# A recurrence and a routed expert layer on one core: the second state part made directly, tanh in two halves, x products, weight pieces and low parts moved

## The reference

```python
def step(h, xt):
    m = jnp.concatenate([xt, h], axis=-1) @ weight + bias     # (64, 512) @ (512, 512)
    c = jnp.tanh(m[:, 256:])
    g = jax.nn.sigmoid(m[:, :256] + 1.0)
    h_new = g * h + (1.0 - g) * c
    return (h_new, h_new)
...
gate_logits = gate_in @ gate_w + gate_b      # from means over steps of x
# two experts of four for each batch; a mask by step for experts 1 and 2
h = gelu(context_c @ ew1[e] + eb1[e]); y = h @ ew2[e] + eb2[e]
out = out + w_be[:, e][:, None, None] * mask[e][None, :, None] * y
shared = gelu(context_c @ sw1 + sb1) @ sw2 + sb2
return x + out + shared
```

## Time and profile before

| | us |
|---|---|
| median of 3 runs | 661.3 |
| the profiled execution | 663.13 |
| its span in the trace | 661.4 |
| TensorE busy | 642.6 (97%) |
| VectorE busy | 415.1 (63%) |
| ScalarE busy | 314.5 (48%) |
| GpSimd busy | 259.9 (39%) |

### The profile page before, as it was taken

How to read it: one execution, slowest core, us unless ns; L and a number is a source line. 1 busy time by engine, 2 the same in 40 slices (tenths; PEclk the granted TensorE clock), 3 DMA queues, 4 the chain that set the end, 5 groups by cost and what they waited for, 6 DMA issues and landing times.

```text
span 661.4 us, 16521 instructions
## 1 busy us (share of the span) xinstructions
PE 642.6 (97%) x5828; PEld 557.7 (84%) x5828; DVE 415.1 (63%) x947; ACT 314.5 (48%) x537; POOL 259.9 (39%) x514
## 2 busy tenths in 40 slices
PE   7799999999999999999999999999999999999995
PEld 4699888888888888888878888888888899999995
DVE  5788987556566655668747644554456785555554
ACT  5454454343443343444647544444446664554460
POOL 1467775544554454433345333123311443311300
PEclk9999999999999999999999999999999999999998
DMA  7510210000000000000002100000001310000006
GB/s 258 205 53 10 58 49 18 0 1 0 0 0 0 0 0 0 1 1 2 1 2 81 48 0 0 0 0 0 0 0 58 94 58 0 0 0 0 0 1 255
DMA packets 7751, 20.74 MB, mean 31 GB/s; under 512 B 800, under 2 KB 1056, under 8 KB 7200
## 3 DMA queue, kind: packets, MB, share of 16 engines
q1 hardware_dynamic: 7424, 19.59, 8.6%
q10 hardware_dynamic: 288, 0.64, 0.3%
HBM read 16.03 MB, written 4.19 MB: 31 GB/s over the span
## 4 chain that ended last, share of the span: by engine, by line
PE 92%; DVE 3%; DMA 1%; issue 1%; ACT 1%; POOL 1%; DVEq 0%; SPq 0%; ACTq 0%; POOLq 0%
PE zy L882 56%; PE hp L882 37%; DMA acc<-in_x 1%; DVE d_t L552 0%; DVE d_t L550 0%; POOL g_lo L370 0%; ACT uc L407 0%; DVE acc L827 0%; DVE h_b L555 0%; DVE h_r L540 0%; DVE y_all L755 0%; DVE h_b L542 0%; ACT g_hi L426 0%; DVE first L559 0%; DVE w_buf L533 0%
## 5 line engine op out<-in xcount | busy, mean ns | idle before, releaser
L527 DVE TENSOR_TENSOR g_lo<-g_f,g_hi 128x512 fp32r<-128x512 f32 (+2 forms) x172 | 127.7, 743 | 156.1 <-ACT g_hi L426 153.8
L882 PE MATMUL zy<-g_hi,w_buf 128*128 128x512 f32 (+2 forms) x736 | 186.6, 375 | 0.5 <-issue 0.5
L426 ACT ACTIVATE g_hi<-g_f 128x512 fp32r<-128x512 f32 (+2 forms) x184 | 109.9, 597 | 152.2 <-PE zy L882 151.8
L419 ACT ACTIVATE g_f<-hp,first 128x512 f32<-128x512 f32 (+3 forms) x188 | 122.9, 654 | 117.8 <-PE hp L882 113.2
L882 PE MATMUL hp<-shared_buf,w_buf 128*128 (+1 forms) x720 | 173.6, 376 | 0.0
L882 PEld LDWEIGHTS hp<-shared_buf,w_buf 128*128 128x128 f32 x720 | 135.0, 188 | 19.0 <-issue 0.3
L882 PEld LDWEIGHTS zy<-g_hi,w_buf 128*128 128x128 f32 x736 | 132.1, 188 | 19.7 <-ACT g_hi L426 0.7
L882 PEld LDWEIGHTS zy<-h_b,y_all 128*128 128x128 bf16 x3072 | 93.9, 98 | 21.5 <-issue 13.1
L882 PE MATMUL zy<-g_lo,w_buf 128*128 128x512 f32 (+2 forms) x368 | 107.6, 373 | 0.9 <-POOL g_lo L370 0.9
L882 PE MATMUL zy<-h_b,y_all 128*128 128x64 bf16 x3072 | 102.7, 193 | 5.8 <-DVE h_b L555 5.3
L882 PE MATMUL hp<-x_hl,w_buf 128*128 (+2 forms) x432 | 104.9, 378 | 0.7 <-POOL x_hl L312 0.7
(11 more groups left out here) (126 smaller groups left out, 455.2 us busy)
## 6 DMA issues: line engine op xcount, KB each, us to landing
stage<-in_w_exp SPq DMA_DIRECT2D x40, 256.0 KB, 2.9
out_y<-acc SPq DMA_DIRECT2D x2, 1376.0 KB, 4.7
acc<-in_x SPq DMA_DIRECT2D x1, 2048.0 KB, 7.7
acc<-in_x SPq DMA_DIRECT2D x1, 1536.0 KB, 10.0
out_y<-acc SPq DMA_DIRECT2D x1, 1344.0 KB, 5.5
acc<-in_w SPq DMA_DIRECT2D x1, 512.0 KB, 4.7
acc<-in_x SPq DMA_DIRECT2D x1, 512.0 KB, 6.9
acc<-in_w ACTq DMA_DIRECT2D x1, 512.0 KB, 5.6
```

What stands on the lines that cost most here:

```text
L419: act.activation(raw_of(j, n, keep), hp[j % 2][:, 0:n], ACT.Gelu_apprx_tanh, bias=par[:, S_B1 + e * NCH + j:S_B1 + e * NCH + j + 1]).then_ ...
L426: act.activation(chunk_of(j, n, keep)[0], raw_of(j, n, keep), ACT.Copy).then_inc(ghi_done, 1)
L527: dve.tensor_tensor(lo, raw_of(j, n, keep), hi.bitcast(F32), ALU.subtract).then_inc(glo_done, 1)
L882: return pe.matmul(out_, lhsT=lhsT, rhs=rhs, start=start, stop=stop, skip_group_check=True)
```

## The change

- The second part is subtracted directly, h - h_b[:, 0] into bfloat16, ahead of h_r, in all steps. It no longer waits for h_r.
- The state products go through m in the order 2, 3, 0, 1 (`C_FIRST`), so the columns of c are complete first; in steps 0 to 11 (`APART`) that raises `c_done`, ScalarE makes the tanh of c and of g as two instructions, and the cell's first instruction waits for c's alone.
- In group 0 the x products stand in steps 0, 1, 2, 3 (one each) and 4 (two), 5, 6 (one each), directly behind the state products; in group 1 one in every step. At step 0 the high parts of x are used first and the low ones behind a wait for POOL. POOL makes the low part of x of step 15 before its last sum of group 0.
- Weight pieces 5, 6, 7 move from steps 5, 6, 7 to 6, 8, 9.
- VectorE makes the low parts of chunks 66, 67, 68 (`DVE_LOW`) after 2, 5 and 8 of the gather copies; POOL leaves them out.

```diff
+APART = GT + QT
+C_FIRST = [2, 3, 0, 1]
+PIECE_AT = {0: 0, 1: 1, 2: 2, 3: 3, 4: 4, GT - 2: 5, GT: 6, GT + 1: 7}
+X_PARTS = [[[0], [1], [2], [3]], [[0, 1], [2], [3], []]]
+DVE_LOW = {6: 2, 7: 5, 8: SLOTS}
...
+            pool.wait_ge(xa_hi, GT)
+            x_low(2 * GT - 1)
             head_low(GT - 2)
             add_h(GT - 1, GT - 1)
-            pool.wait_ge(xa_hi, GT)
-            x_low(2 * GT - 1)
...
             for c in range(T - QT, NS * NCH):
+                if c - T + QT in DVE_LOW:
+                    continue
                 n = width(c // NCH)
-                if c == T - QT:
+                if c == T - QT or c - 1 - T + QT in DVE_LOW:
                     pool.wait_ge(glo_done, c)
...
+            def tanh(s, i, buf, apart=False):
+                if apart:
+                    act.wait_ge(c_done, s + 1)
+                    act.activation(uc[:, 1], zb[:, buf, 1, :, i % QT, :], ACT.Tanh).then_inc(tanh_c, 1)
+                    act.wait_ge(z_done, s + 1)
+                    act.activation(uc[:, 0], zb[:, buf, 0, :, i % QT, :], ACT.Tanh).then_inc(tanh_done, 1)
...
-                piece_high(i)
+                if i in PIECE_AT:
+                    piece_high(PIECE_AT[i])
...
                 gelu_chunk(q, j, E, width(q))
+                if s in PIECE_AT:
+                    piece_high(PIECE_AT[s])
...
                 dve.wait_ge(h_done, s + 2)
+                dve.tensor_tensor(h_b[:, 1], h, h_b[:, 0], ALU.subtract).then_inc(h2_done, 1)
                 dve.tensor_tensor(h_r[:], h, h_b[:, 0], ALU.subtract).then_inc(hr_done, 1)
                 dve.wait_ge(hr_done, s + 2)
-                dve.tensor_copy(h_b[:, 1], h_r[:]).then_inc(h2_done, 1)
                 dve.wait_ge(h2_done, s + 2)
...
+                if apart:
+                    dve.wait_ge(tanh_c, s + 1)
+                else:
+                    dve.wait_ge(tanh_done, s + 1)
                 dve.wait_ge(h_done, s + 1)
                 dve.tensor_tensor(d_t[:], h_f[:, i % 2], uc[:, 1], ALU.subtract).then_inc(d_done, 1)
                 dve.wait_ge(d_done, s + 1)
+                if apart:
+                    dve.wait_ge(tanh_done, s + 1)
...
+                for j, upto in DVE_LOW.items():
+                    for s in range(at, upto):
...
+                        last = dve.tensor_copy(dst, tokens_of(x_hl, ORDER[1], bs[s]))
...
+                    at, c = upto, T - QT + j
+                    dve.wait_ge(glo_done, c)
+                    split_lo(c // NCH, c % NCH, width(c // NCH))
...
+                if low:
+                    for k in range(K):
+                        for w in range(2):
+                            mm(o, wx[:, w, k, c], x_hl[:, 0, k, bass.ds(s, QT), :], False)
+                    pe.wait_ge(xs_done, low)
+                    for k in range(K):
+                        mm(o, wx[:, 0, k, c], x_hl[:, 1, k, bass.ds(s, QT), :], False)
+                    return
...
-                    for m in range(2 * K):
+                    for m in C_FIRST:
...
+                        if apart and a == 2 and m == 2 * K - 1:
+                            last.then_inc(c_done, 1)
                 last.then_inc(z_done, 1)
...
+                    if head != 0 and j:
+                        if head == 1 and i == 0:
+                            pe.wait_ge(piece_done, 6)
+                        layer1(q, j, w_of(0), group_src(q), width(q))
+                    if not (last_group and i >= QT):
+                        if i % QT == 0:
+                            pe.wait_ge(seeded, 2 * g + 1 + i // QT)
+                            if head == 0 and i == 0:
+                                pe.wait_ge(x4_hi, 1)
+                            else:
+                                pe.wait_ge(xs_done, s + QT)
+                        for m in X_PARTS[i // QT][i % QT] if head == 0 else [i % QT]:
+                            x_part(s - i % QT + QT, (i // QT + 1) % 2, m, QT if head == 0 and i == 0 else None)
```

More of the change, by code:

```diff
@@ L403, in seed @@
                                bias_z.unsqueeze(2).to_broadcast([P, 2 * K, QT * B]), ACT.Copy).then_inc(seeded, 1)
[L405 to L408, removed]
+            def tanh(s, i, buf, apart=False):
[5 more added lines that the diff above has]
+                else:
+                    act.wait_ge(z_done, s + 1)
+                    act.activation(uc[:],
+                                   zb[:, buf, :, :, i % QT, :], ACT.Tanh).then_inc(tanh_done, 1)
                 if i % QT == QT - 1:
+                    if apart:
+                        act.wait_ge(tanh_c, s + 1)
                     act.wait_ge(tanh_done, s + 1)
@@ L459, in _ @@
             for i in range(GT):
[L460 removed]
+                tanh(i, i, i // QT, True)
                 act.activation(x_hl[:, 0, :, GT + i, :], acc[:, :, GT + i, :], ACT.Copy).then_inc(xa_hi, 1)
@@ L613, in _ @@
             for i in range(GT):
-                cell(i, i, i < 2)
-                piece_low(i)
+                cell(i, i, i < 2, True)
+                if i in PIECE_AT:
+                    piece_low(PIECE_AT[i])
                 for j in first_chunks(i):
@@ L623, in _ @@
                     shared_out(0, yp)
-                cell(s, i)
+                cell(s, i, apart=s < APART)
                 split_lo(q, j, width(q))
+                if s in PIECE_AT:
+                    piece_low(PIECE_AT[s])
                 if s >= GT + QT:
@@ L911, in h_first, with h_part @@
                     for a in range(3 - b):
-                        for m in range(2 * K):
+                        for m in C_FIRST:
                             for k in range(K):
                                 last = mm(zb[:, 0, m // 2, m % 2, 0, :], wh[:, b, k, m * P:(m + 1) * P], h_b[:, a, k], False, b == 2)
+                            if b == 2 and m == 2 * K - 1:
+                                last.then_inc(c_done, 1)
                 last.then_inc(z_done, 1)
-            def h_part(s, i, buf):
+            def h_part(s, i, buf, apart=False):
                 for a, ready in enumerate((h1_done, h2_done, h3_done)):
                     pe.wait_ge(ready, s + 1)
-                    for m in range(2 * K):
+                    for m in C_FIRST:
                         o = zb[:, buf, m // 2, m % 2, i % QT, :]
@@ L998, in steps @@
                     else:
-                        h_part(s, i, i // QT)
+                        h_part(s, i, i // QT, head is not None and s < APART)
                     q, j = chunk_at(g, i)
+                    if head != 0 and j:
[7 more added lines that the diff above has]
+                                pe.wait_ge(x4_hi, 1)
+                            else:
+                                pe.wait_ge(xs_done, s + QT)
+                        for m in X_PARTS[i // QT][i % QT] if head == 0 else [i % QT]:
+                            x_part(s - i % QT + QT, (i // QT + 1) % 2, m, QT if head == 0 and i == 0 else None)
                     if head == 0:
@@ L1007, in steps @@
                             layer1(0, j, w_of(0), group_src(0), width(0), j < 2)
-                    elif j:
-                        if head == 1 and i == 0:
-                            pe.wait_ge(piece_done, 6)
-                        layer1(q, j, w_of(0), group_src(q), width(q))
-                    if not (last_group and i >= QT):
-                        if i % QT == (0 if head is None else 1):
-                            pe.wait_ge(seeded, 2 * g + 1 + i // QT)
-                            pe.wait_ge(xs_done, s - i % QT + QT)
-                        for m in [i % QT] if head is None else ([], [0], [1], [2, 3])[i % QT]:
-                            x_part(s - i % QT + QT, (i // QT + 1) % 2, m)
                     if head != 0 and j == 0:
```

17 lines of the change are left out of this document (9 added, 8 removed).

## The result

| | before | after |
|---|---|---|
| median, runs on the same chip | 661.5 (6 runs, 661.02 to 663.5) | 659.0 (6 runs, 658.96 to 659.06) |
| the profiled execution | 663.13 | 659.06 |
| its span | 661.4 | 657.3 |
| TensorE busy | 642.6 (97%) | 641.0 (98%) |
| VectorE busy | 415.1 (63%) | 420.5 (64%) |

The ratio is 0.995, interval 0.9937 to 0.9962: faster by 0.5%, more than the 0.2% that a measurement of this kernel can tell. The forecast was 656.7 us, with a range of 654.8 to 659.3 that holds the 659.0. The runs of the kernel before lie on two levels, near 661.3 and near 663.0, and its profiled execution is from the upper one; the kernel after has one level.

What follows compares the result with a forecast made beforehand. TensorE was taken to bound the kernel, its long middle full, so only stalls around it could be won. Head 3.0 plus gather 1.6 made 4.6 us, off the median of 661.3: 656.7 us, range 654.8 to 659.3.

Steps and rivals of the forecast that it cites:

- C: Between recurrence and experts: the gather stall stays, its cause not the port or VectorE's low parts late; 658.3 us, chance 0.07.
- F: Steps 0 to 3 and 7: c_done comes late, keeping 0.3 us a step, 1.5 in all; 658.2 us, chance 0.06.
- Gather, 1.6: Between recurrence and experts: VectorE making low parts of chunks 66 to 68 saves 1.6 us, bounds 0.9 to 1.8.
- Head, 3.0: From the start: 2.65 us saved by step 12, about 0.35 more around step 14; bounds 1.2 and 4.2.
- Tanh: Early recurrence steps: halves of 0.30 us, the second 0.2 to 0.28 behind, make step 2's q 0.3 us sooner.
- Rival B: Steps 0 to 3 and 7: tanh halves do not overlap, 0.78 us a pair, 1.0 us less gain; 657.7 us, chance 0.08.
- Step 3's pin: Step 3: weight piece 2, landing at 22.27, holds cell 3 until 23.64, 0.5 us late; step 4's products start at 24.8.
- The wait for x's low part: Step 4: two x products wait for POOL's low part, 2.85 us after the step's start; step 5 starts at 29.1.
- Steps 8 to 11: VectorE takes over as the bound: 4.4 us in steps 8 and 9, 3.67 in 10 and 11; step 12 at 55.5.
- rival D: Steps 5 to 14: VectorE's subtractions and POOL hold each other off, cells 0.3 us longer; about 659.7 us, chance 0.09.
- A: Steps 8 to 11: VectorE does not bind, its instructions beside POOL shrink; head 4.2 us, total 655.5 us, chance 0.16.
- E: Steps 5 to 14: VectorE steps grow, deciding from 0.46 us each; at 0.65 us slower, 663.2 us, chance 0.04.

Runs made afterwards that it cites:

- experiments 2: The kernel before with only the low parts of chunks 66 to 68 moved to VectorE among the gather copies: 661.13 us, ratio 0.9969.
- experiment 4: The kernel before with VectorE waiting for POOL's low parts after the second and fifth gather copy, POOL keeping all low parts: 661.17 us, ratio 0.9995.
- head alone: The changed kernel without the gather part, so POOL makes the low parts of chunks 66 to 68 again: 661.33 us, ratio 0.9965.
- experiment 6: The changed kernel with one piece undone each time: whole tanh 660.0 us, second part copied from h_r 659.07, weight pieces back 658.84, x products back 660.76.

## Why the prediction was right, and where it was not

**The bound** was read rightly: the middle stays full, and a microsecond saved in the head or the gather reaches the last products whole (2.54 and 1.84 make 4.37).

**The last step of the sum failed.** I took 4.6 us, worked out on an execution of 663.13, from a median of 661.3. The miss of 2.3 us is 1.8 of this and 0.5 of the terms: for the profiled execution the forecast was 658.5, and it took 659.06. The stall of the earlier trace rows was priced rightly, but as if each run had it, though the table of the front showed a profiled execution 1.5 us above the highest run of the median. If the lower level is without the stall (experiments 2 and 4), only the head is left there: 661.3 less 2.54, of which the tail hands 0.36 back, is 659.1. Where before lies at 663.0, after's 659.0 is 4.0 us less.

**That 659.0 lies in the range is luck in part.** It is 0.3 us inside the upper end, 659.3, and the gain is 2.3 to 2.5 us where 4.6 was forecast. The upper end was set for costs such as longer VectorE steps beside POOL (head 1.2), a gather stall that stays (C, 658.3) or a late c_done (F, 658.2), and none of these came at that size. A stall that is missing from the runs of the median was on no list.

**Gather, 1.6:** 1.85. I held back the 0.47 "issue" of the earlier trace rows; it went as well. Rival C is out. POOL's 2.83 us outlasted the rest of the train, more than five copies of 0.39 us, and with the train broken it took 0.74. The Trainium skill, "SBUF — State Buffer", SBUF: two separate sides, says that the loser of the shared port waits for the winner's whole instruction. A wait of one copy does not give this row; that one side waits for a whole instruction of the other does agree with the copies of 0.96 and 0.94 us in experiment 4.

**Head, 3.0:** 2.54 (head alone), 2.56 by step 16 counted from step 0. By its steps:
- Tanh: 0.28 us for a half and 0.17 between starts, close to the 0.30 and 0.2 taken. Rival B is out: the pair takes 0.44 us. The Trainium skill's budget ("ScalarE: Activation LUTs", Rules for kernel authors), from which the prediction estimated 0.82 us for the pair, is stated for an activation whose bias is a pointer operand. The tanh here has none and takes 0.28 and 0.39 us; the gelu, which has one, takes 0.48 for 256 columns, near the 0.51 of that budget. But I put the gain in steps 0 to 3 and 7. By step 8 only 0.45 had come, as the pin of step 3 took 0.28 back, and 0.79 more came behind it, where I had VectorE bound by its own work and the tanh of no account.
- The loop: 3.28 to 3.41 less 0.46 is 2.8 to 2.95, not the 2.9 to 3.0 written. Steps 1 and 2 took 2.95 and 3.08.
- Direct part: 0.16 a step in steps 1 to 3, as taken. What I had not looked at is the end of the program, where a gap of 0.36 us appeared; it is not this part's doing alone (experiment 6).
- Step 3's pin: right in kind, mis-sized. Piece 2 came at 22.50 for 22.27, VectorE's low part took 0.90 and d 0.54 us, so step 4 began at 25.24 for 24.8.
- The wait for x's low part: at 28.26 for 27.65, and step 5 at 29.76 for 29.1. Of these 0.61 us, 0.44 come from step 4, which starts later. The other 0.17 is that TensorE starts 3.02 us behind step 4's products and not 2.85: POOL's low part ends 2.88 behind them (28.12), and TensorE starts 0.14 later. POOL's addition ahead of it (L313, at 26.39) takes 0.79 us, no more than before:

```profile
27.13 0.79 POOL L307 TENSOR_TENSOR acc<-acc,first 128x128 f32<-128x128 f32 x1 [1.89 <-DVE h_b L544]
```

- The pin and this wait make the 0.5 us missing at step 12 (2.18 for 2.65), and 0.44 more by step 16 was near the 0.35 taken.
- Steps 8 to 11: cells at 38.85, 42.27, 46.06, 50.45 and 54.14 for 38.2, 41.5, 45.9, 50.3 and 54.0. VectorE did set the pace there (15.88 us from step 8 to 12, I had 16.1, TensorE's work is 14.6). But it did so by another way. I had TensorE idle before the products of steps 10 and 11, and it was not. The first part was there in time, and the third came late: from start to start the state products of steps 8, 10 and 11 took 1.77, 1.79 and 1.97 us instead of 1.41, which is all of the 1.3 us that these steps took over TensorE's work. It is not rival D: the three instructions behind the state take no longer than before (1.22 to 1.50 us against 1.48), and without the direct part the same steps take 15.95 us. Before, the state products lasted too long here as well, 1.66 and 1.65 us in steps 10 and 11.
- Weight pieces: I gave the move no sum of its own; it is worth nothing.
- The order of the x products is the largest piece of the head (1.63 us on TensorE). The prediction had no term for it, only the step starts, so it gave the runs no worth to be held against. Taken back one at a time the four pieces cost 1.63, 1.24, 0.46 and 0.04 us, 3.37 in all, where together they gain 2.54: a piece is worth more with the others in place than a sum of terms gives it.

A, the head at 4.2, and E did not come, nor did F: from the start of step 2's products to the first half of the tanh it took 1.50 us (18.46 to 19.96) where before it took 1.77 (18.93 to 20.70) with 0.16 of stall in it, so c_done brought the 0.11 or so that I had taken as 0.12, and VectorE's steps were not longer by E's 0.3 us.

## What to carry to other kernels

Before taking a saving from a median, ask whether the profiled execution stands on the median: if it lies above all of the timed runs, one of the stalls that you see may be absent in most of them. A saving placed ahead of a later wait is worth no more than that wait leaves of it. Compare the end of the program too: here 0.36 us gained on TensorE did not reach it. Work that needs nothing of the current step, as x's low part here, belongs ahead of the wait for that step.

## What was not expected of the hardware

- GpSimd's subtraction of 256 columns, 0.74 us alone, took 2.83 us beside a train of eight VectorE copies in every trace of before and of head alone, and 0.88 and 0.73 beside a train of six in another kernel, where two of the copies took 0.96 and 0.94 us instead of 0.46. The share of runs at the upper level goes with the chip: 16 of 16, 11 of 13, 4 of 19, and 2 of 6 on the first.
- A gap of 0.37 us among VectorE's last additions stands in six kernels and not in eight others with the same instructions there, and goes with an instruction transfer 0.25 to 0.75 us behind it; the final write of one execution took 5.6 us instead of 4.7. Both are as large as what single edits are worth here, and the cause of neither is shown.
